# The last pair of edge blocks of a graph-attention kernel, in pieces of 13, 9 and 4 steps instead of 13 and 13

## The reference

```python
h = relu(layernorm(x)) @ W_node.T            # [12500, 4 heads, 32]
att = sum(concat([h[src], h[tgt], e]) * a)   # [412500, 4]
att = where(att > 0, att, 0.2 * att)
m = maximum(segment_max(att, tgt), 0.0)
ex = exp(att - m[tgt])
denom = segment_sum(ex, tgt) + (num_edges - deg) * exp(-m)
out = x + segment_sum(ex / denom[tgt] * h[src], tgt)
```

## Time and profile before

| | us |
|---|---|
| median of 3 runs | 4960.86 |
| lowest, highest | 4958.59, 4969.13 |
| the profiled execution's own time | 4962.95 |
| its span in the trace | 4955.9 |

### The profile page before, as it was taken

The page is one execution under the profiler, slowest core; times in us unless marked ns, Lnnn a source line. Parts: engine busy times, 40 slices in busy tenths (PEclk is TensorE's granted clock), DMA queues, the critical chain, the costliest instruction groups (busy, mean ns, idle before and its releaser), DMA issues.

```text
span 4955.9 us, 14358 instructions
## 1 busy us (share of the span) xinstructions
PE 777.3 (16%) x1453; PEld 390.6 (8%) x1453; DVE 2412.0 (49%) x2384; ACT 1368.3 (28%) x1021; POOL 3712.2 (75%) x3530
## 2 busy tenths in 40 slices
PE   5321111111111111111111111111111111111100
PEld 3310000000000000000000000000000000000000
DVE  7337454545445454454544545445454454544543
ACT  7013232222322222222222322223222232222320
POOL 6667777777777777777777777777777777777766
PEclk9555555555555555555555555555555555555555
DMA  7234444343443434434344343433434434343353
GB/s 250 90 132 119 140 123 128 114 137 114 126 125 114 137 114 128 123 115 137 114 127 123 114 136 114 129 121 115 137 114 128 122 115 136 114 131 120 116 170 104
DMA packets 171831, 627.97 MB, mean 127 GB/s; under 512 B 72897, under 2 KB 73666, under 8 KB 155426
## 3 DMA queue, kind: packets, MB, share of 16 engines
q0 software_dynamic: 115936, 252.37, 21.0%
q1 hardware_dynamic: 55874, 375.39, 20.1%
HBM read 382.66 MB, written 244.86 MB: 127 GB/s over the span
## 4 chain that ended last, share of the span: by engine, by line
POOL 70%; issue 24%; another core or an unknown queue 2%; ACT 2%; DVE 1%; PE 0%; DMA 0%; POOLq 0%; ACTq 0%; DVEq 0%; SPq 0%
POOL slots L308 69%; ACT pen L375 1%; DVE pen L482 0%; PE ae L792 0%; DVE slots L496 0%; ACT big L392 0%; ACT slots L391 0%; POOL tdst_scratch L311 0%; ACT R L421 0%; PE wexp L785 0%; DMA state_scratch<-R 0%; DVE V L636 0%; DVE slots L501 0%; DMA cols<-in_cols_dram 0%
## 5 line engine op out<-in xcount | busy, mean ns | idle before, releaser
L308 POOL DMA_INDIRECT slots<-rows_scratch,idx x3224 | 3421.5, 1061 | 1066.5 <-issue 1066.5
L803 PE MATMUL ae<-eab,w_att 128*128 128x416 f32 x992 | 650.6, 829 | 3796.2 <-DMA eab<-in_ea_dram 2539.1
L603 DVE TENSOR_TENSOR z<-slots,big 128x104 f32<-128x104 f32 (+1 forms) x125 | 43.1, 345 | 2116.3 <-DMA slots<-rows_scratch,idx 1887.3
L636 DVE TENSOR_TENSOR_SCAN V<-A,V 128x1848 f32<-128x1848 f32 x248 | 993.7, 4007 | 35.4 <-issue 4.8
L421 ACT COPY R<-V 128x1716 f32<-128x1716 f32 x248 | 777.8, 3136 | 339.1 <-DVE V L636 196.7
L417 ACT ACTIVATE A<-D 128x1848 f32<-128x1848 f32 x246 | 419.7, 1706 | 744.7 <-DVE V L636 410.3
L803 PEld LDWEIGHTS ae<-eab,w_att 128*128 128x128 f32 x992 | 296.0, 313 | 4150.4 <-issue 3384.4
L626 DVE TENSOR_TENSOR V<-slots,wexp 128x1716 f32<-128x1716 f32 x125 | 404.8, 3239 | 22.4 <-issue 21.0
L626 DVE TENSOR_TENSOR V<-slots,extra 128x1716 f32<-128x1716 f32 x123 | 398.2, 3237 | 22.0 <-issue 16.3
L438 ACT ACTIVATE wexp<-D 128x104 f32<-128x104 f32 x62 | 16.2, 261 | 1092.5 <-DVEq L621 628.8
L438 ACT ACTIVATE extra<-D 128x104 f32<-128x104 f32 x61 | 15.9, 261 | 1063.2 <-DVEq L621 631.2
(11 more groups left out here) (168 smaller groups left out, 602.3 us busy)
## 6 DMA issues: line engine op xcount, KB each, us to landing
state_scratch<-R SPq DMA_DIRECT2D x123, 1768.0 KB
eab<-in_ea_dram SPq DMA_DIRECT2D x126, 832.0 KB
slots<-rows_scratch,idx POOLq DMA_INDIRECT x3224
rows_scratch<-slots SPq DMA_DIRECT2D x14, 476.0 KB
tdst_scratch<-eab SPq DMA_DIRECT2D x4, 1612.0 KB
big<-tdst_scratch SPq DMA_DIRECT2D x8, 806.0 KB
big<-in_x_t_dram SPq DMA_DIRECT2D x14, 448.0 KB, 4.3
big<-in_x_dram SPq DMA_DIRECT2D x7, 896.0 KB
```

The source lines that it names most:

```text
L308: pool.indirect_dma_start(buf, None, table, bass.IndirectOffsetOnAxis(ap=index, axis=0)).then_inc(done, 16)
L636: nc.vector.tensor_tensor_scan(V[:, v, :], a_all, V[:, v, :], 0.0, ALU.mult, ALU.add).then_inc(scanned, 1)
L803: last = mm(ps_ae[k][:, 0:KB * Q], w_att[:, a * P:(a + 1) * P], eab[:, k, a * KB * Q:(a + 1) * KB * Q], start=a == 0, stop=a == 3)
```

## The change

The last pair becomes three pieces, `LAST = ((0, 13), (13, 9), (22, 4))`, each a first step and a number of steps. Every piece has its own `gather_end`, `logits`, weights, decay, scan, copy and store; the tiles of the end get three parts and `M` a third buffer (`M_END` says which piece uses which). A piece's `V` is packed to its own width: 132 x 14, 132 x 10 and 132 x 5 columns. Pieces 0 and 2 both use `V[:, 0]`, so piece 2 waits until piece 0 has been copied (`copied >= p + 1`), and the scratch tiles of the end move to `V[:, 1]`. The counts that others wait for (`d_ready`, `val_done`, `copied`, `STORES`) go up by one. `pen_end` is filled by 12 small activations in place of 4. Nothing is changed for the other 123 pairs but the form of the code.

```diff
+LAST = ((0, KB), (KB, 9), (KB + 9, KB - 9))
...
-        v_tail = V[:, 0, :]
+        v_tail = V[:, 1, :]
...
-        STORES = [16 * (PAIRS // 2), 16 * (PAIRS // 2 + 1)]
+        M_END = (1, 0, 2)
+        STORES = [16 * (PAIRS // 2), 16 * (PAIRS // 2 - 1 + len(LAST))]
...
-                    for v in range(2):
-                        sp.wait_ge(copied, p + 1 + v)
-                        a, b = (p * 2 + v) * (KB * ROW), (p * 2 + v + 1) * (KB * ROW)
-                        sp.dma_start(state_rows[:, a:b], R[:, 1, v * KB:(v + 1) * KB, :].rearrange("p t r -> p (t r)")).then_inc(store_dma[1], 16)
+                    for e, (o, n) in enumerate(LAST):
+                        sp.wait_ge(copied, p + 1 + e)
+                        a = (p * PB + o) * ROW
+                        sp.dma_start(state_rows[:, a:a + n * ROW], R[:, 1, o:o + n, :].rearrange("p t r -> p (t r)")).then_inc(store_dma[1], 16)
...
-                    for v in range(2):
-                        act.wait_ge(d_ready, p + 1 + v)
+                    for e, (o, n) in enumerate(LAST):
+                        act.wait_ge(d_ready, p + 1 + e)
+                        u = (p + e) % 2
+                        nc.scalar.activation(w_exp[u][:, 0:H * n], D1[:, u, 0:H * n], ACT.Exp).then_inc(w_ready, 1)
+                        decay(hk(D2_end[:, e, 0:H * (n + 1)]), n + 1)
...
+                        act.wait_ge(scanned, 2 * p + 1 + e)
+                        copy_sums(1, o, e % 2, n).then_inc(copied, 1)
...
-                    for v in range(2):
-                        dve.wait_ge(gather_end[v], 16 * KB)
-                        logits(p, k, 1 - v, v, KB, att_end, att_end, pen_end[:, v:v + 1, :, :], D2_end[:, v, :])
-                        dve.wait_ge(w_ready, p + 1 + v)
-                        if v == 0:
-                            dve.wait_ge(copied, p)
-                        sums(k, v, hk(w_exp[1 - v][:, 0:H * KB]), 2 * p + 1 + v, False)
+                    for e, (o, n) in enumerate(LAST):
+                        u = (p + e) % 2
+                        c = LAST[e + 1][1] + 1 if e + 1 < len(LAST) else COL
+                        dve.wait_ge(gather_end[e], 16 * n)
+                        logits(p, k, u, M_END[e], o, n, att_end[:, e, :], hk(att_end[:, e + 1, 0:H * c]), pen_end[:, e, 0:H * (n + 1)], D2_end[:, e, 0:H * (n + 1)])
+                        dve.wait_ge(w_ready, p + 1 + e)
+                        if e != 1:
+                            dve.wait_ge(copied, p + e // 2)
+                        m = LAST[e - 1][1] if e else KB
+                        sums(k, o, n, e % 2, hk(w_exp[u][:, 0:H * n]), 2 * p + 1 + e, vcols(1 - e % 2, m + 1)[:, :, m:m + 1])
```

More of the change, by code:

```diff
@@ L74, in graph_attention_kernel @@
         pen = sb("pen", [P, PAIRS, H, PCOL], bf16)
-        pen_end = sb("pen_end", [P, 2, H, COL], bf16)
+        pen_end = sb("pen_end", [P, len(LAST), H * COL], bf16)
         pen_a = sb("pen_a", [P, T], bf16)
         att = sb("att", [P, H * PCOL], fp32)
-        att_end = sb("att_end", [P, H * COL], fp32)
-        M = sb("M", [P, 2, H * PCOL], fp32)
+        att_end = sb("att_end", [P, len(LAST) + 1, H * COL], fp32)
+        M = sb("M", [P, 3, H * PCOL], fp32)
         z = sb("z", [P, H * PB], fp32)
@@ L166, in graph_attention_kernel @@
         gather_dma = [sem(f"gather_dma{k}") for k in range(2)]
-        gather_end = [sem(f"gather_end{k}") for k in range(2)]
+        gather_end = [sem(f"gather_end{k}") for k in range(len(LAST))]
         store_dma = [sem(f"store_dma{k}") for k in range(2)]
@@ L343, in body @@
                     k = q % 2 * PB + j
-                    gather(slots[:, k, :], rows[:, :], idx[:, q // 2, k:k + 1], gather_end[j // KB] if at_end(it, q) else gather_dma[q % 2])
+                    done = gather_end[sum(j >= o for o, n in LAST) - 1] if at_end(it, q) else gather_dma[q % 2]
+                    gather(slots[:, k, :], rows[:, :], idx[:, q // 2, k:k + 1], done)
             loop(pool, body)
@@ L566, in _ @@
             nc.vector.scalar_tensor_tensor(get_i[:, :], cnt[:, 1:W + 1], -1.0, pick[:, :], ALU.add, ALU.add)
-            nc.vector.memset(pen_end[:, :, :, 0:1], -BIG)
+            nc.vector.memset(pen_end[:, :, :], -BIG)
             nc.vector.memset(pen[:, :, :, 0:1], -BIG).then_inc(pen_set, 1)
@@ L621, in logits, with sums @@
                 dve.drain().then_inc(d_ready, 1)
-            def sums(k, v, w4, ready, fresh):
-                v4 = vcols(v).rearrange("p (h v) t -> p h v t", h=H)
-                a = k * PB + v * KB
-                nc.vector.tensor_tensor(v4[:, :, :, 1:COL], slots[:, a:a + KB, 0:VAL].rearrange("p t (h v) -> p h v t", h=H),
-                                        w4.rearrange("p h (a t) -> p h a t", a=1).broadcast_to([P, H, HB, KB]), ALU.mult).then_inc(val_done, 1)
-                if fresh:
-                    nc.vector.memset(vcols(v)[:, :, 0:1], 0.0)
+            def sums(k, o, n, v, w4, ready, before):
+                vc = vcols(v, n + 1)
+                a = k * PB + o
+                nc.vector.tensor_tensor(vc.rearrange("p (h v) t -> p h v t", h=H)[:, :, :, 1:n + 1],
+                                        slots[:, a:a + n, 0:VAL].rearrange("p t (h v) -> p h v t", h=H),
+                                        w4.rearrange("p h (a t) -> p h a t", a=1).broadcast_to([P, H, HB, n]), ALU.mult).then_inc(val_done, 1)
+                if before is None:
+                    nc.vector.memset(vc[:, :, 0:1], 0.0)
@@ L630, in sums @@
                 else:
[L631 removed]
+                    if o:
                         dve.drain()
[L633 removed]
+                    nc.vector.tensor_copy(vc[:, :, 0:1], before)
                 dve.drain()
                 dve.wait_ge(a_ready, ready)
[L636 removed]
+                nc.vector.tensor_tensor_scan(V[:, v, 0:VAL * (n + 1)], A[:, 0:VAL * (n + 1)], V[:, v, 0:VAL * (n + 1)], 0.0, ALU.mult, ALU.add).then_inc(scanned, 1)
@@ L647, in body @@
                 if at_end(it, q):
[L648 to L654 removed]
+                    for e, (o, n) in enumerate(LAST):
+                        u = (p + e) % 2
[7 more added lines that the diff above has]
+                        sums(k, o, n, e % 2, hk(w_exp[u][:, 0:H * n]), 2 * p + 1 + e, vcols(1 - e % 2, m + 1)[:, :, m:m + 1])
                     return
                 dve.wait_ge(gather_dma[k], it * (16 * PB * UP // 2) + 16 * PB * (q // 2 + 1))
[L657 removed]
+                one_before = isinstance(it, int) and it == ITERS - 1 and q == UP - 2
+                logits(p, k, k, k, 0, PB, att, hk(att_end[:, 0, :]) if one_before else hk(att[:, :]),
+                       pen[:, ds(p, 1), :, :].rearrange("p a h t -> p (a h t)"), D2[:, k, :])
                 dve.wait_ge(w_ready, p + 1)
@@ L660, in body @@
                 for v in range(2):
-                    sums(k, v, hk(w_exp[k])[:, :, v * KB:(v + 1) * KB], it * (2 * UP) + 2 * q + 1 + v, isinstance(p, int) and p == 0 and v == 0)
+                    sums(k, v * KB, KB, v, hk(w_exp[k])[:, :, v * KB:(v + 1) * KB], it * (2 * UP) + 2 * q + 1 + v,
+                         None if isinstance(p, int) and p == 0 and v == 0 else vcols(1 - v)[:, :, KB:COL])
                 if isinstance(p, int) and p < UP:
```

73 lines of the change are left out of this document (34 added, 39 removed).

## The result

The changed kernel is slower: 4977.75 us against 4967.99 us, medians of 11 runs each; the ratio is 1.0019, 95% interval 1.001 to 1.0028, some 9.4 us. Eleven runs of it give 4967.99, so 7.1 of the 23.7 us between forecast and result lie in that starting point; the sign is wrong all the same. On four other chips, where the experiments ran, the kernel before takes 4461 to 4475 us; on the one where both were timed the change makes no difference that can be measured (ratio 0.9998, 0.9989 to 1.0007). Both findings have to be explained.

The account below looks back on a forecast made before the run. GpSimd's gathers end the kernel, held back by the last pair's 20.7 us chain; 4.2 us from the pieces and 2.6 from the last store give 6.8, so 4960.86 - 6.8 = 4954.1 us, range 4951 to 4969.

Parts of the forecast that it names:

- starting point: Time of the kernel before from which the forecast subtracts its gain: 4960.86 us, given by three runs.
- Piece 0 and piece 1: Last pair's first 13 and next nine steps: piece 0 unchanged; piece 1 starts earlier, at 4790.00, scan done at 4797.78.
- Piece 2: Last four steps of the last pair: no wait for gathers, copy ends at 4804.50 instead of 4808.74, 4.2 us gained.
- The last store: Store after the last copy, 272 KB in place of 884 KB: 2.8 us instead of 5.41, 2.6 us gained.
- What is late next: Kernel's end: VectorE's small-instruction chain starts only 2.2 us earlier, GpSimd 6.8; keeping all the gain depends on VectorE's pace.
- A: The forecast case, end of kernel: GpSimd's gathers stay last, 6.8 us gained, 4954.1 us; chance 0.50.
- slack of 1.3 us: Output groups before the change: VectorE at its steady pace, without waits, would end at 4941.6 against 4942.92.
- 7.00 us pace: VectorE's time per output group, mostly idle time marked "issue"; whether the kernel pays for it was left open.
- C: Rival, VectorE's tail: slow issue begins earlier, at the small-instruction chain; end 7.1 us later, 4968.0 us; chance 0.17.
- D: Rival, last pair: the hand-offs eat the gain, every bound at its bad end leaves 3 us, 4958; chance 0.08.
- landing time of 1.73 us: Last pair: time from a piece's last gather ending to VectorE's start, taken from piece 0 and used for piece 1.
- The bound for a measurable change: Whole kernel's time: a measurement can tell a change from none at about 0.2%, 9.9 us.

Follow-up runs that it names:

- after_again: The changed kernel, unaltered, run beside the kernel before on a second chip: 4461.45 us against 4461.49, ratio 0.9998 (0.9989 to 1.0007).

## Why the prediction was wrong, point by point

*Piece 0 and piece 1.* Right on the first chip, to a tenth: piece 1 was to start 12.46 us after the pair's start and did at 12.51; piece 2 was to start at 20.29 and did at 20.26. The multiplies (2.29 and 1.05 for 2.29 and 1.10), the scans (2.91 and 1.53) and the copies (2.29 and 1.14 for 2.21 and 1.08) have the lengths of the straight lines.

*Piece 2.* Here is the first step that failed: "The multiply follows 0.25 later: 4800.30 to 4801.40", and the copy ending at 4804.50, 26.96 us after the pair's start. It ended at 32.10. The stall in front of L625 (3.58 us), the late weights and 0.90 us in front of the scan make up the 5.1 us. The 4.2 us of gain became a loss of 0.9.

*The last store.* Right: 3.00 us from the copy's end to `s_first` (4820.84 to 4823.84) for a forecast of 2.8, 2.4 us gained where I took 2.6. The second chip agrees (5.44 and 3.00). The Trainium skill's rule cited there gave an estimated 1.4 and is the worse of the two at this place; it stands under the path of transfers that GpSimd issues, and these are issued by SyncE.

*What is late next.* This is the step that cost the sign: the forecast let the gathers stay last, A, and put nothing on VectorE. It counted VectorE's slack of 1.3 us, saw that it starts its chain only 2.2 us earlier, and left open whether the 7.00 us pace "is paid by the kernel". It was: VectorE ended 21.6 us behind the last gather.

*The rivals.* C was the mechanism: the stretch of slow issue begins earlier, VectorE is last. It was priced at +7.1 us with its onset at the start of the small chain; the onset came in piece 2's `logits`, 28 instructions and drains ahead of the old place (L625 to L715), and T rose by 15.0. Its measure of 0.78 us for an instruction or drain fits what was found, 0.77. Its reason for the onset, a position in VectorE's instruction stream, did not come true: 19 instructions and drains more (11 and 8) would have moved the onset by 19, and it moved by 28. I gave it 0.17, with two arguments against. One was that nothing stalled beside another fetched packet of instructions; that hits the trigger and not the stretch. The fetch was indeed not the trigger: in the changed kernel no packet of that queue falls between 4808 and 4814 us, around the first stall, and on the second chip one is fetched in the kernel before between 4280 and 4322 us without any. The other, that the idle time might be something of the profiled execution alone, is not refuted. The medians over 11 runs moved the same way, by 9.4 us, but the record has a span and a granted clock for each of those runs too and doesn't show that they ran free of recording; and the first chip's traces lack most of their semaphore updates, as told above. What was wrong was to use an untested doubt to lower a chance. A (0.50) is what the kernel would have done there without the stretch: 26.96 + 3.00 = 29.96 us to `s_first` against 36.61, 6.65 gained.

*On the other chips* A's mechanism holds (GpSimd is last) but its size doesn't: 2.0 us of T are D's case, in which under 3 us are left. From piece 1's start to the last copy the forecast has 14.50 us, after_again 14.42, and the one block of the kernel before 13.17. The third hand-off costs 1.3 us, and an earlier start must pay it. On the first chip piece 1 started 5.5 us earlier than the old block, on the second 1.15, and the last copy came 0.1 later: all of the 2.34 us there is the smaller store (2.44 less 0.10). The forecast took the landing time of 1.73 us as fixed. It is 1.67 for the last gather of the pair and 5.5 for the one that ends piece 1, when gathers come every 1.25 us behind a 1768 KB store.

*The bound for a measurable change*, some 0.2%, was a little wide: 0.19% was told clearly in 22 runs, and 0.11% just so in 26 on the fourth chip. The starting point was the larger error: a median of 3 runs, 7.1 us below that of 11, where 2 us of scatter had been allowed.

## What to carry to other kernels

When a change adds instructions to an engine that isn't last, work out when that engine ends, at its own observed pace, before counting what the others gain; and give idle time without a releaser a chance in line with its rows, not with one's liking for an explanation. Look first whether the trace can name releasers at all: a page on which transfers have no time to landing lacks semaphore updates, and there the program text has to say whether anything is waited for. A transfer's landing time is not a constant of the transfer: read it at the very place, beside the stores and loads in flight there, and drop loads that nobody reads at the end of a loop. And where work is cut in pieces, look at the order of the pieces' small steps on each helper engine, since a copy ahead of the next piece's weights takes back a good part of what the cut gives.

## What the runs showed of the hardware

The same program runs at two levels on different chips: 4962.95 us for the kernel before in the first trace and 4463.87 in the second. Three things differ in the traces. GpSimd's gathers in the main loop take 1061 ns on the first and 948 ns on the second, while its gathers outside it take nearly the same (979 and 982 ns, 947 and 945). The rows of costs for the kernel before, on the first chip and on the second:

```profile
L308 POOL DMA_INDIRECT slots<-rows_scratch,idx x3224 | 3421.5, 1061 | 1066.5 <-issue 1066.5
```

```profile
L308 POOL DMA_INDIRECT slots<-rows_scratch,idx x3224 | 3056.3, 948 | 982.6 <-issue 982.6
L308 POOL DMA_INDIRECT V<-in_dst_dram,chunk_i x99 | 97.3, 982 | 32.9 <-issue 20.4
L308 POOL DMA_INDIRECT slots<-state_scratch,get_i x98 | 92.6, 945 | 29.9 <-issue 29.9
```

And the first chip has a stretch at the end in which VectorE completes an instruction or drain only every 0.7 to 0.8 us; every trace of the other four chips is free of it (where VectorE has nothing to wait for, a group takes 3.13 us and not 7.00).

Third, the first chip's two traces hold 1.6 semaphore updates per microsecond of the span, the 16 traces of the other chips 14.4. In the main loop, from 2000 to 4200 us, the trace of the kernel before has one every 0.75 us, nearly the pace of an instruction or drain in the slow stretch. Slow stretch and missing updates were found together on one chip and neither on the four others. That makes the recording itself a suspect, for the stretch and perhaps for the slower gathers; it is not shown, since no run here is known to be free of recording, and with it stays open whether the loss would be there in an unrecorded run.

What brings the stretch on is open. It isn't a place in the program (it began in front of L700 before, in piece 2 after), and it doesn't slow the gathers issued beside it (0.94 us each). The Trainium skill, "NOTIFIC — the notification-queue block", section "Overflow: three behaviours, one of which stalls the engine", says that a full queue of records can be set up to hold the engine that writes them until it is read out. A pace by the number of records and not by their work would look like this stretch, and the missing updates say that records were short there; that the engine was held by them no run here shows, since none reached that chip again.

Also unexpected was how well the end repeats within a kind of chip: T of the kernel before was 174.26, and 173.98 without the unread loads on another chip, and `s_first` of three different edits fell within 0.02 us. Differences of one or two microseconds, hopeless in medians that scatter by 5 to 10, can be read there.
